# Places of TensorE's operands modulo 512 bytes in a four-layer graph kernel

## The reference

```python
h = relu(layernorm(x))
x = x + softmax(w, axis=1)[:, :, None] * (h @ Wv)      # layer 0, w from q . (adj @ k)
h = relu(layernorm(x))
x = x + normalised(adj * exp(q @ k.T)) @ v             # layer 1, one head
h = relu(layernorm(x))
x = x + (softmax(scores * 2 * adj) @ v) @ Wo.T + bo    # layer 2, eight heads
h = relu(layernorm(x))
x = x + relu(sum over k of T^k h Wk[k] + bk[k])        # layer 3, three hops, T from adj
```

## Time and profile before

| | us |
|---|---|
| median of 3 runs | 2319.44 |
| lowest and highest of them | 2314.83, 2321.06 |
| span of the profiled execution | 2310.2 |
| TensorE matmul busy in it | 2287.1 |
| VectorE, ScalarE, GpSimd busy in it | 1318.4, 747.8, 700.2 |

### The profile page before, as it was taken

One profiled execution on the slowest core, in us unless ns is written; L12 is line 12 of the kernel. 1 busy time (PEld: TensorE's weight loads), 2 busy tenths in 40 slices (PEclk: granted clock), 3 DMA queues, 4 the chain that ended last, 5 costly groups with the idle time before them and its releaser, 6 DMA issues.

```text
span 2310.2 us, 39569 instructions
## 1 busy us (share of the span) xinstructions
PE 2287.1 (99%) x16015; PEld 1860.6 (81%) x16015; DVE 1318.4 (57%) x2745; ACT 747.8 (32%) x1333; POOL 700.2 (30%) x930
## 2 busy tenths in 40 slices
PE   8999999999999999999999999999999999999998
PEld 5788788888878877888888888888778888888887
DVE  3565565656556555545554445555686757676753
ACT  3332323333233333333333333333433232323221
POOL 2433333343333322233322223332342121212120
PEclk9999999999999999999999999999999999999999
DMA  6323333333333343222232222222353333333330
GB/s 198 77 76 95 109 101 83 93 91 87 95 108 105 97 124 105 61 60 67 80 93 60 60 61 60 72 85 95 95 142 94 98 94 97 95 97 96 96 78 37
DMA packets 173479, 209.01 MB, mean 90 GB/s; under 512 B 64800, under 2 KB 81264, under 8 KB 173296
## 3 DMA queue, kind: packets, MB, share of 16 engines
q1 hardware_dynamic: 173296, 206.48, 32.0%
HBM read 88.91 MB, written 50.37 MB: 60 GB/s over the span
## 4 chain that ended last, share of the span: by engine, by line
PE 93%; DVE 2%; SPq 2%; ACT 1%; issue 1%; DMA 1%; POOL 0%; DVEq 0%; ACTq 0%
PE bank L327 50%; PE bank L317 29%; PE bank L588 4%; PE bank L343 3%; SPq L1406 2%; PE bank L528 1%; PE bank L501 1%; PE bank L307 1%; PE bank L378 1%; PE bank L511 1%; PE bank L294 0%; DVE hs L648 0%; DVE yt L961 0%; ACT g1T L1022 0%; PE bank L409 0%
## 5 line engine op out<-in xcount | busy, mean ns | idle before, releaser
L327 PE MATMUL bank<-w_hi,h3T_hi 128*128 128x512 f32 x768 | 302.4, 394 | 0.0
L327 PE MATMUL bank<-w_hi,h3T_lo 128*128 128x512 f32 x768 | 299.5, 390 | 0.0
L327 PE MATMUL bank<-w_lo,h3T_hi 128*128 128x512 f32 x768 | 299.5, 390 | 0.0
L615 DVE TENSOR_TENSOR Z_lo<-bank,Z_hi 128x512 fp32r<-128x512 f32 x128 | 87.1, 682 | 181.6 <-ACT Z_hi L973 181.3
L987 ACT ACTIVATE hn<-x,stA 128x512 f32<-128x512 f32 x192 | 140.7, 804 | 99.3 <-POOL stA L1214 99.3
L327 PEld LDWEIGHTS bank<-w_hi,h3T_hi 128*128 128x128 f32 x768 | 144.6, 188 | 30.2
L327 PEld LDWEIGHTS bank<-w_lo,h3T_hi 128*128 128x128 f32 x768 | 144.4, 188 | 30.2
L327 PEld LDWEIGHTS bank<-w_hi,h3T_lo 128*128 128x128 f32 x768 | 144.4, 188 | 30.2
L973 ACT ACTIVATE Z_hi<-bank 128x512 fp32r<-128x512 f32 x128 | 76.1, 596 | 251.1 <-PE bank L327 159.6
L1209 POOL TENSOR_SCALAR stA<-stA 128x4 f32<-128x4 f32 x48 | 11.5, 241 | 448.1 <-DVE stA L629 446.9
L615 DVE TENSOR_TENSOR cT_lo<-bank,cT_hi 128x256 fp32r<-128x256 f32 x128 | 44.7, 409 | 179.7 <-ACT cT_hi L973 179.7
(11 more groups left out here) (222 smaller groups left out, 5824.9 us busy)
## 6 DMA issues: line engine op xcount, KB each, us to landing
hGA<-hs SPq DMA_DIRECT2D x768, 64.0 KB, 2.0
mid<-x SPq DMA_DIRECT2D x32, 1024.0 KB, 4.8
x<-mid SPq DMA_DIRECT2D x32, 1024.0 KB, 5.8
x<-in_x SPq DMA_DIRECT2D x16, 1024.0 KB, 5.7
hGB<-hs SPq DMA_DIRECT2D x256, 64.0 KB, 2.0
out<-x SPq DMA_DIRECT2D x16, 1024.0 KB, 5.4
blk<-in_adj SPq DMA_DIRECT2D x128, 64.0 KB
adj<-in_adj SPq DMA_DIRECT2D x64, 64.0 KB, 3.3
```

What stands on the lines that cost most here:

```text
L327: ins = eng.matmul(b[:], h[l][:, k, ts], W[r][:, k, :], start=(k == 0 and i == 0), stop=(last and k == 3 and i == 2))
L615: return eng.tensor_tensor(lo, src, hi.bitcast(F), ALU.subtract)
```

## The change

Nothing but allocations changes. `shift` allocates an unused tile of 64 bytes times `lines`. Such tiles are put ahead of pairs, and with `before_hi` between the `lo` and the `hi` of a pair. The small tile `stA` moves ahead of `hs` into a part of `pad1`, `pad4` takes its place, and pads at the end of a stage become smaller. The instructions of each engine, their order, shapes and waits are the same in both programs.

```diff
--- before.py
+++ after.py
@@ -97,10 +97,16 @@
         def alloc(ctx, name, shape, dt=F):
             return ctx.enter_context(nc.sbuf_tensor(name, shape, dt))
 
-        def pair(ctx, name, n=4, w=512):
+        def shift(ctx, name, lines):
+            alloc(ctx, name, [128, 16 * lines])
+
+        def pair(ctx, name, n=4, w=512, before_hi=0):
             with ExitStack() as under:
                 raw = alloc(under, name + "_raw", [128, n, w])
-            return {"raw": raw, "lo": alloc(ctx, name + "_lo", [128, n, w], R), "hi": alloc(ctx, name + "_hi", [128, n, w], R)}
+            lo = alloc(ctx, name + "_lo", [128, n, w], R)
+            if before_hi:
+                shift(ctx, name + "_shift", before_hi)
+            return {"raw": raw, "lo": lo, "hi": alloc(ctx, name + "_hi", [128, n, w], R)}
 
         s_pe, s_dve, s_act, s_pool, s_sp = sems("own_pe own_dve own_act own_pool own_sp")
         bank = Banks([root.enter_context(nc.psum_tensor(f"bank{i}", [128, 512], F)) for i in range(8)],
@@ -161,16 +167,23 @@
 
         blk = alloc(root, "blk", [128, 544])
         atc = alloc(root, "atc", [128, 4, 64])
-        alloc(root, "pad1", [128, 224])
+        stA = alloc(root, "stA", [128, 4, 12])
+        alloc(root, "pad1", [128, 176])
         hs = alloc(root, "hs", [128, 4, 4, 4, 32])
         hGA = alloc(root, "hGA", [128, 4, 16, 32])
 
 
         pa = ExitStack()
-        Wm0, Wv0 = pair(pa, "m0"), pair(pa, "v0")
+        Wm0 = pair(pa, "m0", before_hi=1)
+        shift(pa, "shift_v0", 2)
+        Wv0 = pair(pa, "v0", before_hi=2)
+        shift(pa, "shift_h0", 1)
         hT = [pair(pa, "h0T")]
         gT = [alloc(pa, "g0T", [128, 4, 512])]
-        Wa1, Wv1 = pair(pa, "a1"), pair(pa, "v1")
+        shift(pa, "shift_a1", 1)
+        Wa1 = pair(pa, "a1", before_hi=3)
+        shift(pa, "shift_v1", 1)
+        Wv1 = pair(pa, "v1", before_hi=5)
         hn1 = [alloc(pa, f"hnB{i}", [128, 512]) for i in range(4)]
         bv1, crow = alloc(pa, "bv1", [128, 512]), alloc(pa, "crow", [128, 512])
         zrow = alloc(pa, "zrowt", [4, 128])
@@ -178,7 +191,8 @@
         mcol = alloc(pa, "mcolt", [128, 64])
         cols = alloc(pa, "colst", [128, 16])
         ucol, wS, pcol, rcol = (cols[:, i:i + 4] for i in range(0, 16, 4))
-        stA = alloc(pa, "stA", [128, 4, 12])
+        alloc(pa, "pad4", [128, 48])
+        shift(pa, "shift_h1", 1)
         tmp = ExitStack()
         wqk = alloc(tmp, "wqk", [128, 4, 1024])
         wv1 = wqk[:, :, 0:512]
@@ -188,7 +202,7 @@
         urow, crow1 = alloc(tmp, "urow", [1, 512]), alloc(tmp, "crow1", [1, 512])
         bcol, bprod = alloc(tmp, "bcol", [128, 8]), alloc(tmp, "bprod", [128, 4])
         tmp.close()
-        hT.append(pair(pa, "h1T"))
+        hT.append(pair(pa, "h1T", before_hi=1))
         hGB = alloc(pa, "hGB", [128, 4, 16, 32])
         gT.append(alloc(pa, "g1T", [128, 4, 512]))
         unused1 = [alloc(pa, f"unused{i}", [128, 512]) for i in range(2)]
@@ -197,14 +211,20 @@
 
 
         pb = ExitStack()
-        Wq2, Wk2 = pair(pb, "q2w"), pair(pb, "k2w")
+        Wq2 = pair(pb, "q2w", before_hi=1)
+        shift(pb, "shift_k2", 2)
+        Wk2 = pair(pb, "k2w", before_hi=2)
+        shift(pb, "shift_h20", 1)
         hT2 = [pair(pb, "h2T0")]
         QQ = alloc(pb, "QQ", [128, 4, 512])
-        Wv2, Wo2 = pair(pb, "v2w"), pair(pb, "o2w")
+        shift(pb, "shift_v2", 1)
+        Wv2 = pair(pb, "v2w", before_hi=3)
+        shift(pb, "shift_o2", 1)
+        Wo2 = pair(pb, "o2w", before_hi=5)
         KK = alloc(pb, "KK", [128, 4, 512])
         a2 = [alloc(pb, f"adj2{i}", [128, 4, 128]) for i in range(2)]
         sm = [alloc(pb, f"sm{i}", [128, 24]) for i in range(4)]
-        alloc(pb, "pad2", [128, 928])
+        alloc(pb, "pad2", [128, 928 - 16 * 16])
         hT2.append(pair(pb, "h2T1"))
         VV = alloc(pb, "VV", [128, 4, 512])
         bv2, bo2 = abf[:].rearrange("p g t n -> p (g t n)"), blk[:, 0:512]
@@ -216,7 +236,10 @@
 
 
         pc = ExitStack()
-        W3 = [None, pair(pc, "w31"), pair(pc, "w32")]
+        W3 = [None, pair(pc, "w31", before_hi=1)]
+        shift(pc, "shift_w32", 2)
+        W3.append(pair(pc, "w32", before_hi=2))
+        shift(pc, "shift_h30", 1)
         with ExitStack() as under:
             wv3, awb = alloc(under, "wv3", [128, 4, 512]), alloc(under, "awb", [128, 2, 512])
             bvb, sc3 = alloc(under, "bvb", [128, 512]), alloc(under, "sc3", [128, 512])
@@ -224,19 +247,22 @@
         yt = [alloc(pc, f"yt{i}", [128, 512]) for i in range(2)]
         bsum = alloc(pc, "bsumt", [128, 512])
         alloc(pc, "pad3", [128, 512])
-        W3[0] = pair(pc, "w30")
-        Z = [pair(pc, "Z0")]
+        shift(pc, "shift_w30", 1)
+        W3[0] = pair(pc, "w30", before_hi=3)
+        shift(pc, "shift_z0", 1)
+        Z = [pair(pc, "Z0", before_hi=5)]
         T = [{"hi": alloc(pc, f"Thi{i}", [128, 4, 128], R), "lo": alloc(pc, f"Tlo{i}", [128, 4, 128], R)} for i in range(2)]
         zc, ec3, al, rs = (alloc(pc, n, [128, 4, 64]) for n in ("zct", "ec3", "alt", "rst"))
         si = alloc(pc, "sirows", [128, 4, 128])
         bones = alloc(pc, "bones", [128, 128])
         tt = alloc(pc, "ttt", [128, 4, 64])
         alloc(pc, "pad5", [128, 128])
-        hT3.append(pair(pc, "h3T1"))
+        shift(pc, "shift_h31", 1)
+        hT3.append(pair(pc, "h3T1", before_hi=1))
         Z.append(pair(pc, "Z1"))
         bkb = alloc(pc, "bkb", [128, 3, 512])
         junk = alloc(pc, "junk", [128, 2, 512])
-        alloc(pc, "pad6", [128, 2560])
+        alloc(pc, "pad6", [128, 2560 - 16 * 18])
         arow = alloc(pc, "arowt", [128, 2, 512])
         pc.close()
```

## The result

The changed kernel takes 2354.19 us (2352.51 to 2354.40, 4 runs), the kernel before 2319.03 us (2314.83 to 2321.06, 4 runs). The ratio is 1.0158 with an interval of 1.0146 to 1.017, so the change makes the kernel slower by 35 us. The profiled execution of after spans 2350.7 us, 40.5 us more than the 2310.2 of before. In the later experiments the kernel before had medians of 2312.6 to 2314.4 us; against these the loss is 40 us, as between the two spans. One of the ten executions of the later kernel changed_256 took 4711.73 us, which no trace explains; its ratio goes without it, and its median is 2313.80 us without it and 2313.85 with it.

The account below looks back on a forecast made before the run. TensorE bounds the kernel: a count of float32r matmuls times an unchanged start-to-start distance. The 2310.2 us span plus 0 for the change, and 9.2 us around it, gave 2319.4; likeliest 2319 us, range 2306 to 2345.

Parts of the forecast that it names:

- the slower rival: Float32r matmuls: differing places keep load and stream from their steady distance; 5.8 ns on 7221 of 8671 pairs, 2362 us; chance 0.14.
- the count: TensorE: 8832 float32r matmuls of 128 x 512 at 226.7 ns from start to start, 2002 us, 87% of the span.
- The 9.2 us around the span: Added to the 2310.2 us span to reach 2319.4, the median of the three runs shown.
- The 13.4 ns: Each float32r matmul's distance of 226.7 ns over the 213.3 of 512 columns at 2.4 GHz; 118 us in all.
- I take 226.7 ns for all 8832, unchanged: Float32r matmuls on TensorE: moved places leave the distance from start to start as it was, no change; chance 0.75.
- The two sets of rows: Matmul without a load beside it (388 ns against 389) and fp32 rows (429 ns each), read as showing that places don't matter.
- The upper bound from the burst: Starts behind a burst of small matmuls, 232.5 ns apart, bound the possible cost at 5.8 ns more per float32r matmul.
- The faster rival: Float32r matmuls: streamed and loaded slices meet in memory, and apart they don't; 79 us less, 2241 us; chance 0.11.
- Cover of the other engines: VectorE, ScalarE, GpSimd and DMAs at new places: idle time hides any slowdown; 0, with 1.7 us to both sides.
- The partial forms: Only some place differences are dear or cheap: 6 to 10 us more (2325 to 2329) or 11 to 19 less (2300 to 2308).
- The sign named for the slower rival: Chain rows of 60 matmuls at 13.7 to 14.0 us, group means 394 ns and more, above all v2w and layer 3.

Follow-up runs that it names:

- changed_256: The changed kernel with its shifts of 64 to 320 bytes made 0 or 256 bytes; 2313.85 us, ratio 1.000 to the kernel before.

## Why the prediction was wrong

The forecast was 2319 us with a range from 2306 to 2345; the time was 2354.19. The mechanism that came true is nearest to the slower rival's, to which I gave 0.14.

**What bounds the kernel, and the count: right.** 8832 matmuls times the change of the distance gives the change of the span, 40.6 and 40.5 us, and for each kernel tried the same product is within 2.2 us of the difference of the medians. The 9.2 us around the span were misread, as said above; the sum came to the right median of before by it all the same, because the term was taken from that median.

**The step that failed** is "The 13.4 ns thus go with the type float32r, not with the place", and with it "I take 226.7 ns for all 8832, unchanged". The first half is true: fp32 has 429.2 ns at each place and bf16 215.8. The second half doesn't follow. All rows that I had were at equal places, so they could show only that the extra goes with the type there, and not that it would be the same elsewhere. It goes with both: for 128 stationary and 512 moving columns 226.7 ns at a difference of 0 modulo 256, 228.8 to 236.7 at the others. The fp32 rows were also misread in one point, which the sum doesn't use: the 16 rows from 64.91 us are 8 matmuls, two rows each, so that 429 ns is half an fp32 matmul, and float32r is nearly four times as fast as fp32, not twice.

**The two sets of rows.** The duration of 388 ns without a load against 389 with one was read as a sign that the two reads don't meet, and with that as independence of the place. The bench with one stationary column bears out that the amount loaded is no cost, and its distance still differs with the place (228.9 and 231.7). What those rows had left out is the distance: the matmul at 99.88 us is followed by a wait, so its row has no next start to measure.

**The upper bound from the burst** was the right row. Behind small matmuls the distance was 232.5 ns at equal places, 5.8 more; the change's mean is 231.74, 4.6 more than before's mean and 5.0 more than 226.7. The rival's price was 43 us, of which 40.5 came; its 2362 us stood on the median of 2319.4, and the span of 2310.2 with 43 us would have been 2353.2 against 2350.7. I had said against it that those rows show "nothing moved in memory". That counted far too much: they showed that 226.7 is a value that the series must first reach, and a kernel that holds it through nearly all of 8832 matmuls can lose it.

**The rival's wording was half right.** It said that the change of the difference disturbs the step again and again, and counted 7221 of 8671 pairs. The kernels with one constant difference lose 32 and 47 us, and differences changing by 256 bytes lose nothing; change by itself is worth some 10 us of the 40. Nor do the matmuls at one place keep their 226.7 ns among others: in the trace of after those with equal slices of their own have 231.3 ns on the mean (1195 pairs), those whose stream meets the loaded slice at one place 230.4 (1401), both taken modulo 512. The loss spreads over nearly all 8832 with 4.6 ns, where the rival had 5.8 ns on 83% of them. That the products, 40.6 and 43 us, are near each other is in part luck.

**The faster rival** fell: in no series of 512 columns did a place give less than 226.7 ns.

**Cover of the other engines: right.** Their busy times moved by 1.5 us at most, TensorE's ten waits went from 16.9 to 16.1 us.

**The partial forms** came as a pattern, not as a size: groups part by tile (13.87 and 13.99 us by the parity of h3T), the group h1T_lo,a_hi at 402 ns and this one, which had 390 before:

```profile
L353 PE MATMUL bank<-v_hi,h1T_lo 128*128 128x512 f32 x256 | 99.5, 389 | 0.0
```

Both have a difference of 192 modulo 256, and their distances are 238.2 and 226.9 ns. So within a mixed series the loss of one matmul does not follow from its own difference, and no difference stays free of loss by rule. The sign named for the slower rival, rows of 60 at 13.7 to 14.0 us, came (13.87 to 14.00); its group means of 394 and more where they were 389 came for some groups, and not for v2w_hi,h2T_hi (393).

The rule of the Trainium skill that I had cited, on the page "TensorE: Matmul & The Clock Gate" (section "Part 2: What happens when you issue a matmul"), has two ports for weights and moving operand, from which I concluded that places could not matter. The measurements decide against this use of it: 226.7 to 236.7 ns by place. The same page's distance, N/2.4 + 2.5 ns or 215.8 ns for 512 columns, is what bf16 took here, and what float32r took at no place.

**What stays open** is what in the chip makes the distance of float32r depend on the relative place, why the period is 256 bytes, why 16 stationary columns and streams of 448 and 256 have their cheap place elsewhere, and what sets the loss of a single matmul in a mixed series. The kernel with all tiles moved together by 64 bytes was not tried; the bench has it at 226.7 ns.

## What to carry to other kernels

In a kernel that is one long series of float32r matmuls of 128 stationary and 512 moving columns, keep the two tiles at the same place modulo 256 bytes; a pad of 64 or 128 bytes between them cost this kernel 1.4 and 2.0% of its time. Don't carry this to other widths unmeasured: in the bench 256 moving columns were 6.7 ns faster 192 bytes apart than at one place. When a cost appears only for one type or shape, that doesn't clear the parameter that was the same in all rows: look for a row where it differs, and if there is none, widen the range by the nearest disturbed row. And when a long series runs at a value that it reaches only after a few slower steps, ask what may keep it from getting there before asking what may speed it up.

## What the runs showed of the hardware

From the benches, whose granted clock is 1.00, the 2.4 GHz level (the first series of each, which begins with distances of 427 ns, is left aside):

- The distance of float32r matmuls of 128 x 128 by 512 depends on the relative place of moving and stationary slice modulo 256 bytes: 226.7 ns at 0, 228.9 at +64, 231.7 to 233.3 at +128, 233.3 at +192, and up to 236.7 at +4 and +240. bf16 (215.8) and fp32 (429.2 for each of a matmul's two rows) are the same at +0 and +192.
- It is periodic in time, with periods of one to several matmuls. At equal places the 226.7 ns come only after 6 to 10 matmuls, and a single fp32 matmul between two series was enough to lose them. bf16 has its 215.8 ns from the first distance on, fp32 its 429.2 from the second.
- The loss hardly depends on how many stationary columns are loaded (228.3 to 232.6 ns for 1 to 96 columns at +0 and +192), yet the cheap place does (+32 with 16 columns, 226.7 against 231.7 at +0), and so does it on the columns streamed (256: 113.3 at +192, 120.0 at +0).
